# A hybrid transformer layer on one core: the next batch's input normed during the last scores

## The reference, cut to what matters

```python
x = x + attn_a(layernorm(x), Wq, Wk, Wv, Wo)        # 16 heads of 16, rotary, causal softmax
x = x + ffn(layernorm(x), w_gate, w_up, w_down)     # 256 -> 768 -> 256, silu(gate) * up
x = x + attn_b(layernorm(x), maa_*, Wr, Wk, Wv, Wo, decay, gate, u, ln_g, ln_b)   # RWKV-6 recurrence
x = x + ffn(layernorm(x), w_gate, w_up, w_down)

def layernorm(x): m = mean(x); v = var(x); return (x - m) / sqrt(v + 1e-5)
```

## Time and profile before

| | us |
|---|---|
| median of three runs | 3459.59 |
| the profiled execution | 3464.64 |
| its span, from first to last instruction | 3462.9 |
| PE busy | 2969.8 (86%) |
| DVE busy | 2420.4 (70%) |
| POOL busy | 1415.2 (41%) |
| ACT busy | 1311.7 (38%) |

### The profile page before, as it was taken

The page is one execution under the profiler, slowest core; times in us unless marked ns, Lnnn a source line. Parts: engine busy times, 40 slices in busy tenths (PEclk is TensorE's granted clock), DMA queues, the critical chain, the costliest instruction groups (busy, mean ns, idle before and its releaser), DMA issues.

```text
span 3462.9 us, 47013 instructions
## 1 busy us (share of the span) xinstructions
PE 2969.8 (86%) x17088; PEld 1839.3 (53%) x17088; DVE 2420.4 (70%) x4593; ACT 1311.7 (38%) x2721; POOL 1415.2 (41%) x1596
## 2 busy tenths in 40 slices
PE   2397989989898888988889898898988989899898
PEld 1135565365653566445663457635576355653667
DVE  4474787657875677857878468784687747876566
ACT  0173314722246222553226431364313633146222
POOL 0223463335622356224552246422463335633355
PEclk9698999999999999999999999998999989999999
DMA  3700024000330004200050002400024000240000
GB/s 130 112 2 13 19 38 81 2 13 19 49 71 14 1 19 71 48 14 10 19 94 16 13 10 40 88 2 14 15 42 81 2 13 19 38 81 2 1 1 13
DMA packets 70610, 114.96 MB, mean 33 GB/s; under 512 B 9451, under 2 KB 62731, under 8 KB 64187
## 3 DMA queue, kind: packets, MB, share of 16 engines
q1 hardware_dynamic: 67091, 110.72, 16.2%
q10 hardware_dynamic: 3264, 0.79, 0.1%
HBM read 74.69 MB, written 33.65 MB: 31 GB/s over the span
## 4 chain that ended last, share of the span: by engine, by line
PE 49%; DVE 25%; POOL 13%; issue 5%; ACT 4%; DMA 2%; SPq 0%; DVEq 0%; ACTq 0%; POOLq 0%
PE PB L1411 7%; PE PB L1395 6%; PE PB L1381 6%; DVE mxp L1071 5%; PE PB L1483 4%; PE PB L1468 4%; PE PB L1420 4%; DVE arena L1250 4%; PE PB L1525 3%; DVE attn L993 3%; DVE arena L1259 2%; PE PB L1560 2%; ACT arena L824 2%; POOL hl L677 2%; PE PB L1550 2%
## 5 line engine op out<-in xcount | busy, mean ns | idle before, releaser
L824 ACT ACTIVATE arena<-PB 128x512 f32<-128x512 f32 (+3 forms) x1536 | 657.2, 518 | 471.8 <-PE PB L1395 423.8
L1071 DVE TENSOR_REDUCE mxp<-PB 128x1 f32<-128x512 f32 (+3 forms) x1216 | 723.0, 651 | 149.8 <-PE PB L1384 95.9
L1381 PE MATMUL PB<-arena 96*128 96x512 bf16 (+3 forms) x1536 | 462.0, 342 | 50.0 <-DMA arena<-parts 31.9
L1395 PE MATMUL PB<-arena 99*128 99x512 bf16 (+3 forms) x1536 | 447.1, 338 | 44.5 <-DMA arena<-augT 25.1
L677 POOL TENSOR_TENSOR hl<-arena,hh 128x512 fp32r<-128x512 f32 x192 | 251.5, 1310 | 362.9 <-ACT hh L851 361.2
L657 POOL TENSOR_SCALAR_AFFINE_SELECT arena<-arena 128x512 f32<-128x512 f32 x256 | 162.4, 635 | 453.9 <-ACT arena L824 423.8
L1468 PE MATMUL PB<-xh,wgu 128*128 128x512 f32 x768 | 317.9, 414 | 32.9 <-DVE xl L1119 17.2
L1411 PE MATMUL PB<-arena 128*32 128x512 f32 (+3 forms) x3072 | 330.6, 505 | 2.3 <-POOL arena L657 2.3
L1468 PE MATMUL PB<-xl,wgu 128*128 128x512 f32 x768 | 310.0, 404 | 0.1
L1381 PEld LDWEIGHTS PB<-arena 96*128 96x128 bf16 x1536 | 151.2, 100 | 282.5 <-DVE mxp L1071 96.1
L1655 PE MATMUL PB<-arena 128*128 128x128 f32 x1792 | 234.5, 282 | 57.7 <-DVE arena L1250 48.3
(11 more groups left out here) (140 smaller groups left out, 5544.7 us busy)
## 6 DMA issues: line engine op xcount, KB each, us to landing
arena<-parts SPq DMA_DIRECT2D x112, 256.0 KB, 9.3
parts<-arena SPq DMA_DIRECT2D x192, 128.0 KB
arena<-parts SPq DMA_DIRECT2D x16, 768.0 KB, 17.2
arena<-in_x SPq DMA_DIRECT2D x16, 512.0 KB, 4.5
arena<-parts SPq DMA_DIRECT2D x16, 512.0 KB, 19.5
xres<-in_x SPq DMA_DIRECT2D x16, 512.0 KB, 4.2
out<-xres SPq DMA_DIRECT2D x16, 512.0 KB, 14.3
wgu<-arena SPq DMA_DIRECT2D x2, 768.0 KB, 4.5
```

Of the source, the lines that this page charges most:

```text
L824: act.activation(pt[:, U % 3, h, 0:n], bank(b, "score", t)[:, 0:n], ACT.Exp, scale=DH ** -0.5).then_inc(act_emptied, 1)
L1071: dve.reduce_max(mxp[:, k // 2 % 2, hs[0]:hs[-1] + 1, col:col + 1], bank(b, "max", t)[:, 0:n * len(hs)].rearrange("p (h n) -> p h n", n=n) ...
L1381: last = mm(ps, qst[0:AUG, i // 4, HG * (k // 2) + h, 128 * (i % 4):128 * (i % 4) + 128], kst[0:AUG, s0 // HALF, HG * (k // 2) + h, 0:n], ...
L1395: mm(ps[:, 0:n], kst[0:AUG + 3, j // 4, h, 128 * (j % 4):128 * (j % 4) + 128], qst[0:AUG + 3, f, h, HALF - n:HALF], start=True, stop=True) ...
```

## The change

It has four parts.

1. **x0.** The next batch's x is loaded at the start of the batch, right behind the batch's own x, and not after `out_proj(0)`. DVE does all of ln0 (both halves) in one block at the end of its list for the scores, behind `den(6)` and ahead of the residual of `out_proj(0)`. The result overwrites `x0`, and PE turns it from there at the same places as before. The four pieces in FFN1 and mix go. The two `ln_scale(0, ...)` move on POOL to step 161.
2. **over_sums(6)** stands in step 161 ahead of the mask of unit 44, not behind it.
3. **ln_scale(1, b, 0)**, the power of layer norm 1, stands ahead of the last mask (unit 47), not behind it.
4. **AUG_STEP[7]** goes from 153 to 154: the turn of the last maxima stands one unit later in PE's list, and with it `ROWS_AT[7]` goes from 152 to 156.

The diff:

```diff
--- before.py
+++ after.py
@@ -97,7 +97,7 @@
     return next(t for t, n in enumerate(DONE) if n > s)
 
 
-AUG_STEP = [min(BLOCK_END[k] + AUG_AT, NMAX + 1) for k in range(2 * NG)]
+AUG_STEP = [min(BLOCK_END[k] + AUG_AT, NMAX + 2) for k in range(2 * NG)]
 UNIT_STEP = [step_of(HG * U + HG - 1) for U in range(NG * len(UNITS))]
 OUT_AFTER = [LAST_UNIT[k] + (3 if k < 2 * NG - 2 else 2) for k in range(2 * NG)]
 DEN_STEP = [UNIT_STEP[OUT_AFTER[k]] + 4 for k in range(2 * NG - 2)]
@@ -571,8 +571,10 @@
                 for b in range(NB):
                     x_in_again(b)
                     if b + 1 < NB:
-                        wait_filled(sp, b, "o", 0)
+                        if b == 0:
+                            wait_filled(sp, 0, "ln0", 3)
                         x0_in(b + 1)
+                    if b + 1 < NB:
                         parts_store(b + 1, range(4))
                         wait_filled(sp, b, "kv", KV_ORDER[-1])
                         sp.wait_ge(s_chain, 14 * (b + 1))
@@ -660,14 +662,18 @@
                     for t in range(STEPS):
                         if t in BLOCK_END:
                             max_parts(BLOCK_END.index(t))
+                        if t == O_STEP:
+                            over_sums(2 * NG - 2)
+                            if ahead:
+                                ln_scale(0, b + 1, 0)
+                                ln_scale(0, b + 1, 1)
+                        if t == STEPS - 1:
+                            ln_scale(1, b, 0)
                         for U in DIAG_UNITS:
                             if UNIT_STEP[U] == t:
                                 mask_unit(U)
                         if t in DEN_STEP:
                             over_sums(DEN_STEP.index(t))
-                        if t == O_STEP:
-                            over_sums(2 * NG - 2)
-                    ln_scale(1, b, 0)
                     over_sums(2 * NG - 1)
 
 
@@ -681,8 +687,6 @@
                         h_low_part(1, 0, e)
                         if e == 0:
                             ln_scale(1, b, 1)
-                        if e == 5 and ahead:
-                            ln_scale(0, b + 1, 0)
                         if e == 8:
                             ln_scale(2, b, 0)
                     wait_filled(pool, b, "dn1", 3)
@@ -697,8 +701,6 @@
                             wait_emptied(pool, b, "mix", 4 * mi + 2 * f + c)
                             a = xf[:, s % 4, c, :]
                             pool.tensor_tensor(a, a, xT[:, c, 1 + HALF * f:1 + HALF * f + HALF], ALU.add).then_inc(mix_added, 1)
-                        if ahead and s == 4:
-                            ln_scale(0, b + 1, 1)
 
                     wait_emptied(pool, b, "w", 3)
                     src, at_, n = wdec, 0, 512
@@ -1000,7 +1002,7 @@
                     ln_means(0, p, f, stats0, mv0)
 
                 def x0_norm(p, f):
-                    ln_norm(0, p, f, x0, spare, mv0, rstd0)
+                    ln_norm(0, p, f, x0, x0, mv0, rstd0)
 
                 def rotary(p, e):
                     f = e // 2 % 2
@@ -1109,6 +1111,11 @@
                         if t in DEN_STEP:
                             den(DEN_STEP.index(t))
                     den(2 * NG - 2)
+                    if ahead:
+                        x0_means(b + 1, 0)
+                        x0_means(b + 1, 1)
+                        x0_norm(b + 1, 0)
+                        x0_norm(b + 1, 1)
 
                     def x_low(k, s, ns):
                         xh, xl, _, _, _ = ffn_sets[k]
@@ -1143,8 +1150,6 @@
                         for e in range(2 * NM):
                             if e == SECOND_AT[k]:
                                 x_low(k, s, (2, 3))
-                            if e == 5 and k == 1 and ahead:
-                                x0_means(b + 1, 0)
                             if e == 1 and k == 1:
                                 dve.wait_ge(x_loaded[1], 16 * (b + 1))
                                 residual("o", 2, 0)
@@ -1162,8 +1167,6 @@
                                 remainder(b + 1, 3 + e)
                             if k == 3 and ahead and 3 <= e < 7:
                                 low(b + 1, 1 + e)
-                            if e == 6 and k == 1 and ahead:
-                                x0_norm(b + 1, 0)
                             if e == 9 and k == 1:
                                 ln_norm(2, b, 0, xres, xn, mv, rstd)
 
@@ -1212,11 +1215,8 @@
                     mixed(4)
                     if ahead:
                         pair(low, b + 1, 0)
-                        x0_means(b + 1, 1)
                     mixed(5)
                     mixed(6)
-                    if ahead:
-                        x0_norm(b + 1, 1)
                     mixed(7)
                     mixed(8)
                     if ahead:
@@ -1335,7 +1335,7 @@
                         last.then_inc(filled, 1)
 
                 def transpose_x0(p, f):
-                    transposes(p, "ln0", spare, ln_out[0], 1, (2 * f, 2 * f + 1))
+                    transposes(p, "ln0", x0, ln_out[0], 1, (2 * f, 2 * f + 1))
 
                 def qk_item(p, e):
                     m, f, q = unit(e)
```

## The result

| | before | after |
|---|---|---|
| median of four runs, us | 3459.38 | 3375.77 |
| lowest to highest | 3454.15 to 3463.0 | 3373.62 to 3377.67 |
| the profiled execution | 3464.64 | 3373.62 |
| its span | 3462.9 | 3371.8 |

The changed kernel takes 0.9758 of the time [0.9746, 0.977]: 83.6 us less by the medians, where 74.6 were forecast. The two profiled executions are 91.1 us of span apart, since that of before was slower than each of the four runs and that of after was the fastest of its four. The experiments came in three groups, each with its own runs of the kernel before (medians 3456.82, 3457.41 and 3457.47), so a difference in us between a version and the changed kernel is uncertain by some 2 us beyond the intervals.

A forecast was written before the change was run, and what follows sets the result against it. PE was taken to bound the kernel, holding 49% of the chain of waits; 28.6 + 15.9 + 4.0 + 12.0 + 14.1 = 74.6 us off 3464.64 gave 3390.0 profiled, 3385 for the median, range 3367 to 3412.

The forecast's parts named there:

- over_sums(6): Step 161: PE's 3.58 us idle ahead of out_proj(0) goes whole, 28.6 us over eight batches.
- The clock in out_proj: Its 32 multiplications run at the full clock once the idle gap ahead is gone: 72.46 to 56.56, 15.9 us.
- The block on DVE at nothing: End of scores: statistics and eight norms of x0 end by 693.4, covered by 0.2 to 2.0 us, so no cost.
- a residual right behind the block: Sign of a wrong forecast: DVE's residual starts right at the block's end with PE's product long done.
- The rule on the shared port pair: In the DVE block, each power or mask on POOL can hold up a norm by its own length; no us rest on it.
- The power ahead of the last mask: Way to FFN1: layer norm 1's power starts 0.72 earlier; 0.5 us per batch taken, 4.0 in sum.
- The turn of the last maxima: End of the scores: waits of PE and ACT around the turn shrink, 1.5 us per batch, 12.0 in sum.
- The rival that the rows land late: Ahead of unit 40: rows land as late as before, 12.0 missing; with less from the clock 3405, chance 0.13.
- PE waiting for these rows ahead of unit 40: Sign of a wrong forecast: PE waits for DMA arena<-augT before unit 40.
- The pieces that leave FFN1: From out_proj(3)'s end to the second down: 2.0 us less in seven batches, 14.1 in sum.
- Batch 7 as the control: Without a next batch its FFN1 is already the new one: 34.64 us against batch 3's 36.66.
- The mix stage at nothing: Removing ln0's other half from mix gains nothing, as PE is busy for 65.29 of 66.60 us.

The follow-up runs named there:

- sums_alone: The kernel before with over_sums(6) ahead of the mask of unit 44 and nothing else; 3425.5 us, 0.9906.
- turn_alone: The kernel before with AUG_STEP[7] at 154 instead of 153 and nothing else; 3449.23 us, 0.9969.
- norm2_first: The changed kernel with the first power of layer norm 2 in FFN1 ahead of POOL's subtraction h_low(8), not behind it; 3372.07 us, 0.9751.
- no_power: The changed kernel with ln_scale(1, b, 0) behind the last mask again; 3384.58 us, 0.979.
- no_x0: The changed kernel without the x0 part, ln0 back where it was; 3398.7 us, 0.9831.
- half_in_mix: The changed kernel with the second half of ln0 and its power back in the mix stage, x0 still in place; 3377.83 us, 0.9773.
- power_alone: The kernel before with ln_scale(1, b, 0) ahead of the last mask and nothing else; 3456.74 us, 0.9999.
- longer16: The changed kernel with sixteen more, unused statistics instructions of x0 inside the new block on DVE; 3397.9 us, 0.983.

## Why the prediction was right, point by point

**over_sums(6): right.** No idle time before L1420 in any batch (the prediction's L1422 and L1437 are L1420 and L1435 in the changed kernel). With the turn, an ordinary batch's scores fall by 5.1; forecast were 3.58 + 1.5. sums_alone shows 3.8 of it in batch 1 and turn_alone 1.5.

**The clock in out_proj: right in size and place.** 15.1 against 15.9, 7.17 us a batch at a clock of 1.00, with 31.0 us less at 1.2 GHz in this stage. The record of the clock has it fall 0.4 to 0.8 us into the multiplications in five batches and 0.5 to 1.7 us ahead of them, still in PE's idle time, in three; the prediction had it behind the idle time each time. What the term left out is that such a gain is not kept by itself: alone, part 2 lost 8.2 us, about half of it, in FFN1 and FFN3. With the other parts beside it these losses are mostly gone. Why the stretches at half clock fall better in the changed kernel is open: I can show where they fall, not foretell it.

**The block on DVE at nothing: right.** Forecast were 8.1 us from its start at the slow durations; it took 6.7 (671.30 to 677.99), since four of the eight norms took 1.35 together. 1.75 of cover is left in batch 1, near the 2.0 given for fast norms. The sign that I had named as a wrong one, a residual right behind the block, is there in part: PE's first half was ready at about 677.5 (673.91 and half of 7.17), and the first residual came 0.4 later; it delayed nothing, since the second still waited 1.75. The load of x0 cost nothing that the trace shows: PE's wait ahead of the first scores of batch 0 is 21.33 us, before 22.08.

**The rule on the shared port pair: it holds for some of POOL's work.** The Trainium skill (SBUF — State Buffer, "Who interferes with whom") says that a VectorE instruction that uses both ports of the pair and a GpSimd one exclude each other, and that the one that starts second blocks for the whole of the other. The traces agree in size for the subtractions and masks, where the first norm waits: four norms take 1.61 when they start 0.14 into a mask of 0.64, 2.25 when they start 0.14 into a subtraction of 1.27, and 3.25 beside two subtractions in a row (norm2_first). For the power they do not: the four norms beside the power of 1.06 (675.21) take 1.35, no longer than the 1.38 with POOL idle. So the powers, each of which the prediction let hold up a norm, held up none.

**The power ahead of the last mask: right in sum by luck, as two errors cancel.** This is the term that was mis-sized. The bound of 0.72 counted the mask and not the 0.42 in which POOL waited for ACT ahead of it, although the row was shown. The norm starts 1.05 earlier, and the way to FFN1 shrinks by 7.6 alone and 6.1 here. But the first pairs with `out_proj(2,3)` took 2.2 more, with 4.6 us more at half clock, so the net is 3.9 against 4.0; no_power gives this stage 2.3 back, so the 2.2 belong to this part. Left out of the changed kernel it costs 8.8 in the whole time.

**The turn of the last maxima: right in the scores.** 1.5 a batch forecast, 1.5 measured alone; of the 12.0 only 7.6 are in the time of turn_alone. The rival that the rows land late falls: 2.27 from issue to use. The sign that I had named as a wrong one, PE waiting for these rows ahead of unit 40, is there in all eight batches, but with 0.18 to 0.36 us, 1.75 in sum.

**The pieces that leave FFN1: the second down right (34.65, forecast 34.6), the sum too small.** 12.8 us went up to FFN1's last pair and 5.4 from there to the mix stage, together 18.2 against 14.1. The way to the mix stage has the clock at half for less time (51.2 us before, 30.7 after); that this is why more went is likely and not shown. Batch 7 as the control could not show that. no_x0 puts the value of part 1 at 22.9, where 14.1 was forecast; alone it is 17.8.

**The mix stage at nothing: right,** by half_in_mix, and by PE, which keeps the same distances for 82 us from the start of mix (769.81 before, 747.70 after). What the prediction missed is behind it.

**Missed: 6.3 us in the recurrence.** No term of the sum stands for it. PE's idle time ahead of one of its lines, L1655, in us and times, before:

```profile
  DVE arena L1250: 48.3, 70
```

after:

```profile
  DVE arena L1250: 39.2, 58
```

and in norm2_first:

```profile
  DVE arena L1250: 49.7, 72
```

The same work in the recurrence of batch 1, where the pair on DVE starts 85.5 us after the start of mix both times. Before:

```profile
855.31 2.42 DVE L1250 TENSOR_TENSOR arena<-arena 64x512 f32<-64x512 f32 x2
...
855.74 1.43 POOL L724 TENSOR_TENSOR arena<-arena 128x512 f32<-128x512 f32 x1 [1.44 <-PE PB L1655]
...
857.78 1.16 PE L1655 MATMUL PB<-arena 128*128 128x128 f32 x8 [1.08 <-DVE arena L1250]
```

And after, where a stretch at 1.2 GHz ends just there:

```profile
833.23 1.44 DVE L1250 TENSOR_TENSOR arena<-arena 64x512 f32<-64x512 f32 x2
...
834.27 1.55 POOL L726 TENSOR_TENSOR arena<-arena 128x512 f32<-128x512 f32 x1 [1.55 <-PE PB L1655]
...
834.72 1.03 PEld L1655 LDWEIGHTS PB<-arena 128*128 128x128 f32 x8
```

Before, POOL's multiplication starts 0.43 into the pair on DVE, ahead of the second of the two, and the pair takes 2.42. After, PE is slower just ahead, so POOL's multiplication starts 1.04 into the pair, when the second already runs; the pair takes 1.44, and PE does not wait. The stage takes 159.1 to 159.6 in the kernels of the table with up to 5.0 us at 1.2 GHz in it, and 158.2 to 158.6 in those with 6.8 or 7.5. That the collision is the cause is read from the traces; no run held the clock and moved the collision alone. The Trainium skill (the same section) names this pair: a VectorE instruction with two inputs in SBUF contends with a GpSimd one that reads SBUF. The 2.42 before agrees with it, and the 1.44 after with the rule that the one that starts second waits.

**The sum.** The span fell by 16.5 us more than the 74.6: 6.7 in the scores (the disturbed batches of before), 4.1 in FFN1, 6.3 in the recurrence, 0.3 in FFN3, less 0.8 for the clock in `out_proj` and 0.1 for the power. By the medians, which hold less of the first, it is 9.0. Batch 1 takes 406.0 us, not 416.4: the distance shrinks by 10.4, where less than 5 would have felled the forecast.

## What to carry to other kernels

Move work off an engine that another one waits for into a stretch where it idles, and check the cover at slow durations; where an in-order list holds a ready instruction behind one that still waits, count that wait as part of the gain. A stage without the moved piece, such as the last batch of a loop, prices its removal before it is tried, but only up to the next place where the clock changes. Judge an edit of 1 us a batch in the kernel where it will stay: here one was worth nothing alone and 8.8 us with the others.

## What the runs showed of the hardware that was not expected

- A gain can bring new stretches at 1.2 GHz behind it. power_alone shortened the way to FFN1 by 7.6 us, had 308.1 us at 1.2 GHz against 277.8 before, and took the same time.
- Less time at half clock is not always less time. In mix and recurrence norm2_first has 34.1 us of it and the changed kernel 58.8, and the stage is 5.4 us longer; in the whole kernel it has 193.0 against 212.8, with medians of 3372.07 and 3375.77.
- Four norms of 128x256 on DVE take 1.35, 1.61, 2.25 or 3.25 us, by what POOL does beside them: a power, a mask, one subtraction, two subtractions. Removing the wait of 1.88 us ahead of them cost 1.00 of it again.
- Work that comes late on DVE can reach POOL by way of a PSUM bank. In longer16 two residuals came 2.7 us later, PE waited 0.48 and 1.10 us for the banks that they free, and POOL's masks came 1.66 later.
